# Partial maxima of two octets folded by one transposition in every odd slot, instead of one each slot

## The chip, the core and the metric

One Trainium2 chip, of which the kernel uses one core. The metric is the device time of one launch in microseconds (us), on the slowest core, here the only one. A core has five engines that run their own instruction lists and wait for one another on semaphores: TensorE (PE in the profile, with its weight loads as PEld), VectorE (DVE), ScalarE (ACT), GpSimd (POOL) and SyncE (SP, which here only issues DMAs; SPq and ACTq are the DMA issues of SP and ScalarE).

## The reference

Sixteen batches of 128 rows and 1024 columns pass through a gated cross attention and a gated feed-forward layer with low-rank experts. Cut to what matters here:

```python
def reference(x, ctx, ...):
    # x, ctx: (16, 128, 1024) float32
    y = layernorm(x)
    q, k, v = proj(y, Wq, bq), proj(ctx, Wk, bk), proj(ctx, Wv, bv)   # (b, 16 heads, 128, 16, 4)
    q, k, v = interfere(q), interfere(k), interfere(v)                # mixes the 4 parts of a head
    scores = einsum('bhqdm,bhkdm->bhqkm', q, k) / sqrt(16)            # 64 (head, part) pairs a batch
    weights = softmax(scores, axis=3)                                 # over the 128 keys
    out = einsum('bhqkm,bhkdm->bhqdm', weights, v)
    x = x + tanh(g_xattn) * (out.reshape(b, s, dm) @ Wo.T + bo)
    return x + tanh(g_ffn) * ffn(layernorm(x))                        # base product + 8 experts of rank 64
```

## The kernel before

**The program as a whole.** Three stages follow one another, all bound by matmuls. First the projections of keys, values and queries (up to about 523 us of the profiled execution), then attention (about 523 to 930 us), then the feed-forward part. Each product of two float32 matrices is made of three matmuls of rounded halves (hi by hi, hi by lo, lo by hi).

**Octets and slots.** The 64 (head, part) pairs of a batch are handled in octets of eight, so there are `OCTS` = 128 octets. Attention is written as a row of slots, and each engine has its own loop over the slots `s`. What an engine does for octet `o` stands in a fixed slot: TensorE makes the first scores and the fold of octet `s` in slot `s`, and the second scores of octet `s - LAG` with `LAG` = 3.

**Why scores are made twice.** Softmax needs the maximum over keys, but scores stand with keys on partitions. So:

- `first_pass(o, i)` (line 1734) makes the scores of half `i` of an octet, two matmuls into PSUM bank `one_bank[i]`. `first_pass(s + 1, 0)` is issued in slot `s`, `first_pass(s, 1)` at the start of slot `s`.
- VectorE's `partial_max(o, i)` (line 1924) turns 32 by 32 squares of it and takes negated maxima into the tile `part`, 16 numbers a partition for each half (s_part).
- TensorE's `fold(o)` (lines 1738 to 1742) waits for both halves and transposes `part` into the first 32 rows of `one_bank[1]`, 32 rows by 128 columns. VectorE's read of the fold (lines 1961 to 1966) reduces them into `negmax`, one number for each of 32 by 32 (s_max). The next octet's `first_pass(s + 1, 1)` writes the same bank, and so waits for s_max.
- GpSimd (lines 2017 to 2026) splits `negmax` into a hi and a lo row in `neg`: a copy (line 2022) and a subtraction (line 2024).
- SP's `place_max(o)` (lines 1644 to 1647) stands in slot `o + 1` and copies `neg` into two further rows of the octet's query tile by DMA (s_neg). Behind it, in each slot, SP issues `load_oct(s + 4)`, three DMAs of keys and queries, and in early slots stores of late queries and loads of `wo` rows.
- `second_pass(o)` (line 1754) makes the scores again with those two rows, so that the maximum is subtracted inside the matmul, four matmuls into `two_bank`. It waits for s_neg and, for each bank, for ScalarE's exponentials of the octet before (line 1870).

**What else TensorE does in a slot.** Every fourth slot (7, 11, 15 to 131, all odd, called values slots below; `half_at(s, 0)` is not None) it issues `values(h)` (line 1771), 64 small matmuls. In the other slots from 16 on it issues `project` (lines 1715 to 1717): two, three and three groups of three matmuls in the three slots between values slots, none in a values slot itself. Slots up to 15 have `late_step` (lines 1784 to 1786) instead: the last five of the query projections' 40 steps each, which the kernel has moved into attention. ScalarE and VectorE evict each late block (lines 1853 and 1957) in slots 3, 6, 9, 13 and 16 (`late_end` + 1), and SP and ScalarE store it. In VectorE's loop the late eviction stands ahead of the read of the fold.

**Order in a slot on TensorE.** In a values slot: `first_pass(s, 1)`, `values`, `first_pass(s + 1, 0)`, `fold(s)`, `second_pass(s - 3)`. In the others: `first_pass(s, 1)`, the first half of the projection or late work, `second_pass(s - 3)`, `first_pass(s + 1, 0)`, `fold(s)`, the rest of that work.

## Time and profile before

| | |
|---|---|
| time, median of 3 runs | 1318.53 us |
| lowest and highest | 1314.94 and 1320.28 us |
| the profiled execution: time | 1313.11 us |
| its span (first to last instruction) | 1311.3 us |
| TensorE matmul busy | 1294.1 us, 99% |
| VectorE, ScalarE, GpSimd busy | 57%, 31%, 48% |

The profile is of one execution. Its busy shares are averages over three stages. A busy TensorE is no TensorE at its peak, since the duration of a matmul contains the time in which the next one already runs; what a matmul costs is the distance to the next. The chain of waits gives that distance for each piece of work. TensorE's granted clock is at full speed (its upper level, 2.4 GHz) throughout attention. Idle time of an engine that nobody waits for costs nothing.

### The profile page before, as it was taken

How to read it: one execution, taken by the hardware profiler on the slowest of the kernel's cores; microseconds unless marked ns; L12 is line 12 of the kernel's file. 1: busy time of each engine (PE TensorE's matmuls, PEld its weight loads, DVE VectorE, ACT ScalarE, POOL GpSimd, SP SyncE). 2: the span in 40 equal slices, each digit the busy share in tenths (PEclk: the TensorE clock that was granted, in tenths of full speed). 3: DMA queues.
4: the chain of work that ended last, by engine and by line, in shares of the span. 5: the costliest groups of instructions: out<-in, count | busy, mean ns of one | idle time of the engine just before them, and what ended most of it. 6: DMA issues, size and time to landing. Idle time of an engine off the chain costs nothing.

```text
span 1311.3 us, 22186 instructions
## 1 busy us (share of the span) xinstructions
PE 1294.1 (99%) x8128; PEld 1087.0 (83%) x8128; DVE 742.2 (57%) x1375; ACT 411.2 (31%) x743; POOL 635.4 (48%) x801
## 2 busy tenths in 40 slices
PE   8999999999999999999999999999999999999999
PEld 8888888888878888787888888888788888888887
DVE  6423343468875546576777777777966355254100
ACT  3312221111112222455655555555550121111100
POOL 1899999999962641456665665655600000000000
PEclk9999999999999999999999999999999999999999
DMA  7898764467559997998878878777554514233011
GB/s 248 253 323 212 205 145 146 163 202 211 166 195 245 254 218 214 282 270 249 235 236 231 234 234 223 221 219 222 186 208 95 163 31 121 106 74 104 33 49 48
DMA packets 248077, 244.98 MB, mean 187 GB/s; under 512 B 81568, under 2 KB 182048, under 8 KB 247968
## 3 DMA queue, kind: packets, MB, share of 16 engines
q1 hardware_dynamic: 202416, 196.99, 51.3%
q10 hardware_dynamic: 45552, 46.56, 13.1%
q8 instruction: 65, 1.06, 0.3%
q14 instruction: 44, 0.36, 0.1%
HBM read 152.23 MB, written 83.90 MB: 180 GB/s over the span
## 4 chain that ended last, share of the span: by engine, by line
PE 66%; DMA 2%; ACTq 1%; SPq 1%; ACT 1%; issue 0%; DVE 0%; POOL 0%; DVEq 0%; POOLq 0%
PE bank L171 13%; PE bank L173 13%; PE bank L172 13%; PE bank L1734 5%; PE bank L1754 4%; PE bank L1715 4%; PE bank L1716 4%; PE bank L1717 4%; PE bank L1771 4%; PE bank L1741 1%; ACTq L695 1%; DMA wait_rows<-in_wo_rows 1%; DMA xb<-in_x 1%; DMA q_rows<-wq_own 0%; DMA q_in<-neg 0%
## 5 line engine op out<-in xcount | busy, mean ns | idle before, releaser
L1924 DVE TRANSPOSE_TENSOR_REDUCE part<-bank 128x16 f32<-128x512 f32 x256 | 174.2, 692 | 2.9 <-PE bank L1734 0.5
L1870 ACT ACTIVATE probT<-bank 128x512 f32<-128x512 f32 x256 | 138.8, 595 | 88.3 <-PE bank L1754 84.8
L1715 PE MATMUL bank<-w_hi,oT_hi 128*128 128x512 f32 x256 | 108.1, 422 | 1.2 <-POOL oT_lo L2037 1.2
L729 DVE SCALAR_TENSOR_TENSOR stage_lo<-bank,bias_mixed,stage_hi 128x512 fp32r<-128x512 f32 x46 | 34.5, 751 | 127.1 <-ACT stage_hi L731 127.1
L171 PE MATMUL bank<-place_a,w_hi 128*128 128x512 f32 x256 | 99.7, 390 | 1.7 <-DVE place_a L164 1.7
L1716 PE MATMUL bank<-w_lo,oT_hi 128*128 128x512 f32 x256 | 100.5, 392 | 0.0
L1717 PE MATMUL bank<-w_hi,oT_lo 128*128 128x512 f32 x256 | 100.3, 392 | 0.0
L171 PE MATMUL bank<-w_hi,yT_hi 128*128 128x512 f32 x256 | 99.9, 390 | 0.0
L173 PE MATMUL bank<-w_hi,yT_lo 128*128 128x512 f32 x256 | 99.6, 389 | 0.0
L172 PE MATMUL bank<-place_a,w_hi 128*128 128x512 f32 x256 | 99.6, 389 | 0.0
L172 PE MATMUL bank<-w_lo,yT_hi 128*128 128x512 f32 x256 | 99.6, 389 | 0.0
L173 PE MATMUL bank<-place_a,w_lo 128*128 128x512 f32 x256 | 99.6, 389 | 0.0
L171 PE MATMUL bank<-place_b,place_a 128*128 128x512 f32 x256 | 99.6, 389 | 0.0
L172 PE MATMUL bank<-place_c,place_a 128*128 128x512 f32 x256 | 99.6, 389 | 0.0
L173 PE MATMUL bank<-place_b,place_a 128*128 128x512 f32 x256 | 99.6, 389 | 0.0
L958 POOL TENSOR_TENSOR mixed_sum<-mixed_sum,mixed_part 128x512 f32<-128x512 f32 x64 | 90.8, 1419 | 5.0
L1538 DVE SCALAR_TENSOR_TENSOR raw_d<-bank,gates,raw_d 128x512 f32<-128x512 f32 x32 | 23.9, 746 | 121.2 <-PE bank L173 121.2
L2022 POOL CAST neg<-negmax 32x32 fp32r<-32x32 f32 x128 | 26.0, 203 | 133.4 <-DVE negmax L1965 84.9
L1965 DVE TENSOR_REDUCE negmax<-bank 32x32 f32<-32x128 f32 x128 | 35.7, 279 | 96.2 <-PE bank L1741 96.2
L171 PE MATMUL bank<-place_b,w_hi 128*128 128x512 f32 x216 | 84.5, 391 | 0.0
L172 PE MATMUL bank<-place_b,w_hi 128*128 128x512 f32 x216 | 84.1, 389 | 0.0
L173 PE MATMUL bank<-place_b,w_lo 128*128 128x512 f32 x216 | 84.1, 389 | 0.0
(256 smaller groups left out, 3123.5 us busy)
## 6 DMA issues: line engine op xcount, KB each, us to landing
k_rows<-stage_hi SPq DMA_DIRECT2D x128, 128.0 KB, 2.7
v_pad<-v_out SPq DMA_DIRECT2D x32, 512.0 KB, 2.8
v_place<-v_pad ACTq DMA_DIRECT2D x64, 256.0 KB, 4.2
tin<-in_ctx_cols SPq DMA_DIRECT2D x26, 512.0 KB, 4.0
k_in<-k_rows SPq DMA_DIRECT2D x64, 192.0 KB, 3.0
q_in<-q_rows SPq DMA_DIRECT2D x128, 96.0 KB, 3.3
q_rows<-wq_own SPq DMA_DIRECT2D x81, 128.0 KB, 4.2
raw_d<-x_mid SPq DMA_DIRECT2D x17, 512.0 KB, 3.6
```

The lines of the kernel that those rows point to most:

```text
L171: nc.tensor.matmul(bank_ap, sh, mh, start=(i == 0), stop=False)
L172: nc.tensor.matmul(bank_ap, sh, ml, start=False, stop=False)
L173: last = nc.tensor.matmul(bank_ap, sl, mh, start=False, stop=(i == len(chunks) - 1))
L958: then(pool.tensor_tensor(mixed_sum[:] if m < 3 else cols, mixed_sum[:], mixed_part[:], ALU.add))
L1715: pe.matmul(o_bank[out][:], hi[:, c, :], wo_hi[:, k, cols], start=(k == 0), stop=False)
L1716: pe.matmul(o_bank[out][:], hi[:, c, :], wo_lo[:, k, cols], start=False, stop=False)
L1717: last = pe.matmul(o_bank[out][:], lo[:, c, :], wo_hi[:, k, cols], start=False, stop=(k == KC - 1))
L1734: last = pe.matmul(dst, k_in[slot][0:ROWS, p, :], q_in[slot][0:ROWS, :, p, :], start=True, stop=True, skip_group_check=True)
L1754: last = pe.matmul(dst, k_in[slot][:, p, :], q_in[slot][:, :, p, :], start=True, stop=True, skip_group_check=True)
L1771: last = pe.matmul(v_bank[a][32 * p:32 * p + 32, i * P:(i + 1) * P], v_in[b % 2][:, 4 * (o % NOCT) + p, a, :], probT[o % NPT][:, p // 2, a ...
L1870: act.activation(probT[o % NPT][:, i].rearrange("k a p q -> k (a p q)"), two_bank[i][:], ACT.Exp).then_inc(s_exp, 1)
L1924: dve.tensor_reduce(part[o % NS][:, :, 2 * i:2 * i + 2, :].rearrange("k a p b -> k a (p b)"), one_bank[i][:].rearrange("k (a b t) -> k a b ...
```

## The change

Four edits, all in attention.

- `part` holds two octets, `[P, 2, 2, 4, 4]` in three buffers. `fold` runs in odd slots alone: one transposition of 64 columns for octets `s - 1` and `s`, into the first 64 rows of `one_bank[1]`. VectorE reads both in the odd slot, one reduction for each octet (the second reads rows 32 to 63), and GpSimd splits both there. SP places both in the even slot behind it, ahead of that slot's `load_oct`.
- `first_pass(o, 1)` of an odd octet waits for the partial maxima of the octet before (s_part), that of an even octet for the reads of the fold (s_max), both of them.
- In odd slots that are no values slots, `second_pass` stands behind `first_pass(s + 1, 0)` and `fold(s)` rather than ahead of them.
- VectorE's late eviction stands behind the reads of the fold.

```diff
-            part = [sb(f"part{i}", [P, 2, 4, 4], F32, st) for i in range(NS)]
+            part = [sb(f"part{i}", [P, 2, 2, 4, 4], F32, st) for i in range(NPAIR)]
...
-                    if 1 <= s <= OCTS:
+                    if 2 <= s <= OCTS and s % 2 == 0:
+                        place_max(s - 2)
                         place_max(s - 1)
...
+                        elif o % 2:
+                            pe.wait_ge(s_part, 2 * o)
                         elif o:
                             pe.wait_ge(s_max, o)
...
                 def fold(o):
-                    if 0 <= o < OCTS:
+                    if o < OCTS and o % 2:
                         pe.wait_ge(s_part, 2 * o + 2)
-                        pe.transpose(one_bank[1][0:32, 0:P], part[o % NS][:].rearrange("k a p b -> k (a p b)"),
+                        pe.transpose(one_bank[1][0:64, 0:P], part[o // 2 % NPAIR][:].rearrange("k e a p b -> k (e a p b)"),
                                      ident[:]).then_inc(s_fold, 1)
...
-                    second_pass(s - LAG)
+                    folds = h is None and s % 2 == 1
+                    if not folds:
+                        second_pass(s - LAG)
                     if h is None:
                         first_pass(s + 1, 0)
                         fold(s)
+                    if folds:
+                        second_pass(s - LAG)
...
+                    for o in (s - 1, s) if s < OCTS and s % 2 else ():
+                        dve.wait_ge(s_fold, s // 2 + 1)
+                        if o >= NS:
+                            dve.wait_ge(s_nlo, o - NS + 1)
+                        mine = one_bank[1][32 * (o % 2):32 * (o % 2) + 32, 0:P]
+                        dve.tensor_reduce(negmax[o % NS][:], mine.rearrange("c (i q) -> c q i", i=4), AX.X,
+                                          ALU.min).then_inc(s_max, 1)
                     for j, e in enumerate(late_end):
...
-                    if s < OCTS:
-                        dve.wait_ge(s_fold, s + 1)
-                        if s >= NS:
-                            dve.wait_ge(s_nlo, s - NS + 1)
-                        dve.tensor_reduce(negmax[at][:], one_bank[1][0:32, 0:P].rearrange("c (i q) -> c q i", i=4), AX.X,
-                                          ALU.min).then_inc(s_max, 1)
```

GpSimd's loop changes as VectorE's does: the copy and the subtraction of octets `s - 1` and `s` in odd slots, none in even ones.

TensorE in a values slot, from the fold to the first scores of the next octet's second half. Here `bank7` is `one_bank[1]`, into which fold and first scores both write, `bank0` and `bank1` are `two_bank`; `q_in`, `early_q` and `first_q` are query tiles, `k_in`, `early_k`, `second_k` and `first_k` key tiles. Before:

```order
L1741 MATMUL bank7<-ident,part1 32x128 [waits s_part]
L1754 MATMUL bank0<-q_in4,k_in4 128x2x128 [waits s_exp,s_neg4]
L1754 MATMUL bank0<-q_in4,k_in4 128x2x128
L1754 MATMUL bank1<-q_in4,k_in4 128x2x128 [waits s_exp]
L1754 MATMUL bank1<-q_in4,k_in4 128x2x128
L1734 MATMUL bank7<-first_q,first_k 128x2x128 [waits s_max]
```

Now:

```order
L1745 MATMUL bank7<-ident,part0 64x128 [waits s_part]
L1758 MATMUL bank0<-q_in4,k_in4 128x2x128 [waits s_exp,s_neg4]
L1758 MATMUL bank0<-q_in4,k_in4 128x2x128
L1758 MATMUL bank1<-q_in4,k_in4 128x2x128 [waits s_exp]
L1758 MATMUL bank1<-q_in4,k_in4 128x2x128
L1738 MATMUL bank7<-first_q,first_k 128x2x128 [waits s_max]
```

Nothing moved here; the transposition is wider, and its wait s_max, four matmuls later, now counts two reads.

TensorE two slots later, in the odd slot that is no values slot, from its second half on. Here `bank6` is `one_bank[0]`. Now the order is

```order
L1738 MATMUL bank6<-early_q2,early_k2 128x2x128 [waits s_part,s_kq2]
L1738 MATMUL bank6<-early_q2,early_k2 128x2x128
L1745 MATMUL bank7<-ident,part1 64x128 [waits s_part]
L1758 MATMUL bank0<-q_in6,k_in6 128x2x128 [waits s_exp,s_neg6]
L1758 MATMUL bank0<-q_in6,k_in6 128x2x128
L1758 MATMUL bank1<-q_in6,k_in6 128x2x128 [waits s_exp]
L1758 MATMUL bank1<-q_in6,k_in6 128x2x128
L1717 MATMUL bank5<-w0_hi,oT_hi0 128x512 [waits s_y]
```

where the second scores stood ahead of all of these rows before.

SP, the placing of maxima (`neg`) among the loads of keys and queries. Before:

```order
L1646 DMA early_q3<-neg3 2x32x32 [waits s_nlo]
L212 DMA first_k<-k_rows 96x512 [waits s_two]
L215 DMA first_q<-q_rows 48x512 x2
L1646 DMA q_in4<-neg4 2x32x32 [waits s_nlo]
L212 DMA second_k<-k_rows 96x512 [waits s_two]
L215 DMA early_q1<-q_rows 48x512 x2
L1646 DMA q_in5<-neg5 2x32x32 [waits s_nlo]
```

Now:

```order
L1647 DMA q_in6<-neg4 2x32x32 [waits s_nlo]
L1647 DMA q_in7<-neg5 2x32x32 [waits s_nlo]
L212 DMA k_in4<-k_rows 96x512 [waits s_two]
L215 DMA q_in4<-q_rows 48x512 x2
L212 DMA k_in5<-k_rows 96x512 [waits s_two]
L215 DMA q_in5<-q_rows 48x512 x2
L1647 DMA first_q<-neg0 2x32x32 [waits s_nlo]
```

The even octet's placing moved behind one more slot's loads.

## Rows read from the trace of the kernel before

**Rows 1.** The page: busy us (share of the span) xinstructions, for each engine.
```profile
PE 1294.1 (99%) x8128; PEld 1087.0 (83%) x8128; DVE 742.2 (57%) x1375; ACT 411.2 (31%) x743; POOL 635.4 (48%) x801
```

**Rows 2.** Who waited for whom: TensorE from 522 to 620 us: total, times, longest.
```profile
PE bank L1734 <- DVE negmax L1965: 3.7, 3, 1.7
PE bank L1734 <- DMA q_in<-q_rows: 0.7, 1, 0.7
PE bank L1754 <- DMA early_q<-neg: 0.6, 2, 0.4
PE bank L1734 <- DVE part L1924: 0.5, 1, 0.5
```

**Rows 3.** Chain of waits, start us and us, from a values slot on.
```profile
701.23 0.43 PE bank L1734 x2
701.67 0.11 PE bank L1741
701.78 0.48 PE bank L1754 x4
702.26 0.40 PE bank L1734 x2
...
703.83 0.24 PE bank L1734 x2
704.07 0.11 PE bank L1741
704.18 0.23 PE bank L1715
```

**Rows 4.** One line's instructions, L1741: count, ns min/median/max, first and last start.
```profile
L1741 PEld LDWEIGHTS bank<-ident,part x128: 94/94/96, 526.1 to 917.9; 128*32 128x32 f32 x128
```

**Rows 5.** One line's instructions, L1754, as in group 4.
```profile
L1754 PEld LDWEIGHTS bank<-q_in,k_in x256: 186/190/203, 550.3 to 924.9; 98*128 98x128 f32 x128
```

**Rows 6.** Timeline in and behind a values slot: start us, us, instruction, [idle before <-releaser].
```profile
713.54 0.27 PE L1741 MATMUL bank<-ident,part 128*32 128x128 f32 x1
713.57 0.72 PE L1754 MATMUL bank<-first_q,first_k 98*128 98x256 f32 x4
714.18 0.51 PE L1734 MATMUL bank<-q_in,k_in 96*128 96x256 f32 x2
...
718.36 0.64 PE L1754 MATMUL bank<-early_q,early_k 98*128 98x256 f32 x4
```

**Rows 7.** The same timeline on VectorE.
```profile
713.85 0.28 DVE L1965 TENSOR_REDUCE negmax<-bank 32x32 f32<-32x128 f32 x1 [1.06 <-PE bank L1741]
714.06 1.39 DVE L1924 TRANSPOSE_TENSOR_REDUCE part<-bank 128x16 f32<-128x512 f32 x2
```

**Rows 8.** Timeline on SP's queue, early slots and the stretch of group 6.
```profile
544.38 0.54 SPq L1646 DMA_DIRECT2D q_in<-neg  x1
...
547.26 0.54 SPq L1646 DMA_DIRECT2D q_in<-neg  x1
...
714.90 0.53 SPq L1646 DMA_DIRECT2D early_q<-neg  x1
```

**Rows 9.** DMA issues: KB each, median us from issue to landing.
```profile
v_place<-v_pad ACTq DMA_DIRECT2D x64, 256.0 KB, 4.2
...
yin<-yturn SPq DMA_DIRECT2D x144, 32.0 KB, 1.9
```

**Rows 10.** Chain of waits in early slots: start us, us.
```profile
537.26 0.75 DVE wq_own L1957
538.01 0.20 DVE negmax L1965
538.25 0.51 PE bank L1734 x2
...
551.77 4.30 DMA q_in<-neg
556.12 0.74 PE bank L1754 x4
```

**Rows 11.** Timeline on TensorE at the end of slot 16.
```profile
579.76 0.40 PE L1717 MATMUL bank<-w_hi,oT_lo 128*128 128x512 f32 x1
581.78 0.50 PE L1734 MATMUL bank<-early_q,second_k 96*128 96x256 f32 x2 [1.63 <-DVE negmax L1965]
```

More of the change, by code:

```diff
@@ L1149, in build @@
             NS = 6
-            part = [sb(f"part{i}", [P, 2, 4, 4], F32, st) for i in range(NS)]
+            NPAIR = NS // 2
+            part = [sb(f"part{i}", [P, 2, 2, 4, 4], F32, st) for i in range(NPAIR)]
             negmax = [sb(f"negmax{i}", [32, 32], F32, st) for i in range(NS)]
@@ L1923, in partial_max @@
                     dve.wait_ge(s_one, 2 * o + i + 1)
-                    dve.tensor_reduce(part[o % NS][:, :, 2 * i:2 * i + 2, :].rearrange("k a p b -> k a (p b)"),
+                    dve.tensor_reduce(part[o // 2 % NPAIR][:, o % 2, :, 2 * i:2 * i + 2, :].rearrange("k a p b -> k a (p b)"),
                                       one_bank[i][:].rearrange("k (a b t) -> k a b t", a=2, t=32), AX.X, ALU.max,
@@ L1930, in _ @@
                     if s < OCTS:
-                        at = s % NS
                         partial_max(s, 0)
@@ L2016, in _ @@
                 for s in range(SLOTS):
-                    if s < OCTS:
-                        at = s % NS
-                        pool.wait_ge(s_max, s + 1)
-                        if s >= NS:
-                            pool.wait_ge(s_neg[(s - NS) % KQ], 16 * ((s - NS) // KQ + 1))
+                    for o in (s - 1, s) if s < OCTS and s % 2 else ():
+                        at = o % NS
+                        pool.wait_ge(s_max, o + 1)
+                        if o >= NS:
+                            pool.wait_ge(s_neg[(o - NS) % KQ], 16 * ((o - NS) // KQ + 1))
                         pool.tensor_copy(neg[at][0:32], negmax[at][:]).then_inc(s_nhi, 1)
-                        pool.wait_ge(s_nhi, s + 1)
+                        pool.wait_ge(s_nhi, o + 1)
                         pool.tensor_tensor(neg[at][32:64], negmax[at][:], neg[at][0:32].bitcast(F32),
                                            ALU.subtract).then_inc(s_nlo, 1)
-                        pool.wait_ge(s_nlo, s + 1)
+                        pool.wait_ge(s_nlo, o + 1)
                     h = half_at(s, 5)
```

## The prediction, made before the changed kernel ran

> **What bounds the kernel now.** I read the busy shares first. TensorE has work in 99% of the span, VectorE in 57% [rows 1], so whatever moves the end must lengthen or shorten TensorE's own row of instructions. Then I read who waited for whom: nearly all of TensorE's visible waiting in attention lies before 620 us and sums to some 6 us [rows 2]. Last I read the chain of waits, since a busy share hides two things here. It prices each piece by the distance to the next: a fold costs TensorE 0.11 us, the two matmuls of a half of the first scores 0.24 us, the four of the second scores 0.48 us, a projection matmul 0.23 us. And in a values slot the two matmuls behind the second scores cost 0.40 us instead of 0.24 [rows 3]. That is a wait of 0.16 us which the table of waits doesn't show, because the matmul in front still counts as busy. It is the wait for the read of the fold. The reader should see two things: 128 folds, all on the path, and a wait behind the fold in every values slot that is already not covered.
>
> **Folds removed.** 64 of 128 folds go, at 0.11 us each [rows 3]: 64 x 0.11 = -7.0 us. All of it is on the path, as the chain runs through TensorE there.
>
> **Folds widened.** The remaining 64 load 64 columns instead of 32. The load of 32 columns takes 94 ns [rows 4], that of 128 takes 190 ns [rows 5], so one column costs 1 ns and 64 columns take about 126 ns. It runs beside the matmul in front, which lasts 0.12 us (half of 0.24). So between nothing and 0.03 us each, 0 to 2.0 us in all. I take 0.01 us, which is what sticks out of the cover: +0.6 us.
>
> **The wait in the values slots.** The fold starts at 713.54, TensorE goes on with the next first scores at 714.18 [rows 6]. In between VectorE starts its read at 713.85, needs 0.28 us, and is done at 714.13 [rows 7]. All that TensorE has to do meanwhile is the second scores, 0.48 us, and these don't cover it. Now the same first scores wait for two reads. VectorE's next instruction starts 0.21 us behind the start of a read [rows 7], so the second read ends 0.21 us later at least; if it begins only when the first is done, 0.28 us later. The second reads rows 32 to 63 of the bank, and no instruction in these slots changes rows like that, so no row decides between the ends; I take 0.24 us. Values slots with a next octet are 7 to 123, thirty of them, less slot 15 where a late step of 0.7 us lies behind the fold: 29 x 0.24 = +7.0 us (6.1 to 8.1). This eats what the folds give. The Trainium skill, in "VectorE: DVE Perf Modes", section "Two Vector instructions with no wait between them", states that an instruction whose input starts in another group of 32 partitions than the last one's is held until all earlier ones are finished. By that rule the upper end, 8.1 us, would be the value, and the sum 1.1 us higher; no row here shows it.
>
> **The other odd slots.** There the second scores now stand behind the fold. The read pair needs 0.31 us from the fold's start, 0.21 to 0.28 more, 0.28 and 0.05 us, some 0.9 us. Its cover is the fold, 0.11, the second scores, 0.48, and one group of three projection matmuls, 0.69 us: 1.28 us. So nothing; without the move the cover would be 0.80 us and a tenth would stick out. The fold itself comes 0.48 us earlier, and VectorE's partial maxima of the slot end more than that ahead. Even slots have no fold to wait for. Their first scores wait for partial maxima that are long made. Nothing.
>
> **Placing.** Even octets are placed one slot later. GpSimd's work per pair is the same. SP issues two DMAs in the even slot, 0.53 us each [rows 8], before that slot's loads, and none in the odd one. The loads are needed four slots on (12 us), so their delay is hidden. The window that shrinks is that of the even octets. For those folded in a plain odd slot the second scores come behind all of `values`, 1.9 us of work, so they keep over 5 us. For those folded in a values slot: fold at 713.54, placing issued at 714.90 [rows 8], that is 1.36 us behind; the second scores two slots on start at 718.36 [rows 6], 4.82 us behind the fold. After the change these are later by 0.24 (the longer wait) + 0.24 + 0.11 (first scores and fold put ahead) and earlier by 0.11 (the fold gone in between): 5.30 us. 5.30 - 1.36 = 3.9 us for landing, less 0.1 for the weight load: 3.8 us. What does landing take? Small pieces on the same queue take 1.9 us, and 256 KB on ScalarE's queue 4.2 us [rows 9]; this very DMA took 4.30 us in an early slot [rows 10]. With 26 such slots from 620 us on, the ends are 0 and 26 x 0.5 = 13 us. I take a landing mostly below 3.8 us, because the last load ahead of it on SP's queue is now issued some 3 us before instead of just before, with an occasional longer one: +1.5 us. The Trainium skill, in "DMA: Bandwidth & Descriptors", section "Anatomy of one DMA", gives a fixed cost of about 2.0 us for a DMA (fitted on GpSimd's path) and hardly anything for 8 KB. By that this term would be nothing and the sum 1.5 us lower; the 4.30 us of the row speaks against it for a loaded queue.
>
> **Early slots.** Two visible waits are for a read that stands behind a late eviction: 1.7 us before 538.25, behind VectorE's 0.75 us eviction that itself waited for ScalarE [rows 10], and 1.63 us before 581.78 [rows 11]. The first goes nearly whole, as the reads move ahead of the eviction. In slot 16 there is no fold any more, but the eviction still stands ahead of slot 17's partial maxima, so some 0.3 us remains. A short wait of the first fold for partial maxima goes too. But the early slots are also where SP is slowest: placings come 2.9 us apart there [rows 8], behind loads and stores, and octet 6's landing already holds TensorE up to 556.12 [rows 10]. Octets 4, 6, 16 and 18 would be placed 2 to 3 us later than now. What TensorE gains at 538 it then waits for at 550, and about 1 us more; again some 0.8 us at 556 and 1.5 us around 592 to 600. Sum of this part: -1.7 - 0.2 + 2.6 + 0.8 - 1.4 + 1.3 = +1.4 us. The ends: all waits of these slots that the edits touch go and nothing comes, -4 us; each of the four octets costs 2.5 us net of a gain of 4, +6 us.
>
> **Sum.** -7.0 + 0.6 + 7.0 + 0 + 1.5 + 1.4 = +3.5 us. Lower ends together: -7.0 + 0 + 6.1 + 0 + 0 - 4 = -5 us. The profiled execution took 1313.1 us, 5.4 us below the median of the runs shown (1314.9 to 1320.3). On its own time that is 1316.6 us, on the median 1318.5 + 3.5 = 1322 us.
>
> **The rivals.**
>
> *The placings land too late (slower).* Mechanism: in the slot two behind each values slot TensorE stands before the second scores until the even octet's maxima have landed. It speaks for it that engines of the DMA are mostly busy in attention and that 4.30 us was seen; against it that in the steady slots no wait for `neg` is listed now. At 4.3 us in all of them: 3.5 - 1.5 + 13 = +15 us, 1333.5 us. It leaves the band of no change when those 26 slots wait 0.18 us each on average, a mean landing near 4.0 us.
>
> *The wider fold costs by its columns (slower).* If the fold's 0.11 us is all its own columns, 64 cost 0.22 us and nothing is saved: +3.5 + 7.0 = +10.5 us, 1329 us. Against it: the load of 32 columns, 94 ns, already fits under the matmul in front, and 128 columns follow each other at 0.12 us [rows 3, 5].
>
> *The second read doesn't hold TensorE (faster).* If the pair ended no later than the one read now, or the second scores covered it, the folds' 7.0 us would stay: -7.0 + 0.6 + 0 + 1.5 + 1.4 = -3.5 us, and with the early waits gone as well (-4 instead of +1.4, no late landing) -10.4 us: 1308 to 1315 us. Against it: the chain shows this wait open already, so anything behind it is added.
>
> **How the numbers follow.** A measurement can tell about 0.5%, 6.6 us, from no change: 1311.9 to 1325.1 us. My sum lies inside it, chance 0.57. Late landings 0.23 and the costly fold 0.07 lie above it: 0.30 slower. The last rival far enough to leave the band, with the early waits gone: 0.13 faster. The range leaves out 0.1 at each side: it reaches down to 1312, where the lower ends of all terms lead (-5) and a little beyond, and up to 1334, the full price of the late landings.
>
> **What would show it.** Chain of waits in a values slot: the two matmuls behind the second scores at 0.61 to 0.68 us instead of 0.40. The fold at 0.11 or 0.12 us, 64 times. Two reads with starts 0.21 (or 0.28) us apart. No chain piece through VectorE's eviction at 538 us, but longer pieces of `neg` DMAs at about 550, 556 and 592 to 600 us. In steady slots hardly any wait of line 1758 for `neg`. Wrong would be: a stage much shorter than now by 5 us or more, which would mean that the second read is covered, or waits for `neg` in most of the slots behind a values slot.

## The result

| | median | lowest to highest | runs |
|---|---|---|---|
| before | 1317.21 us | 1314.53 to 1322.11 | 20 |
| after | 1321.92 us | 1318.55 to 1326.70 | 20 |

The ratio is 1.0042, with a 95% interval of 1.0031 to 1.0053: 0.4% slower, 4.7 us by the medians. Forecast was 1322 us and no change that counts, and both held. The sum of +3.5 us was near, but it was made of terms that were not all right: the trace shows two of them too small and two too large.

**The profile after.** The profiled execution took 1321.57 us (span 1319.7). The one of before took 1313.11 us and so lies 4 us below its own median, this one at its median. The two traces therefore differ by 8.4 us where the medians differ by 4.7.

The page's busy times of the changed kernel, against [rows 1]: 64 matmuls fewer on TensorE, and the same busy time.

```profile
PE 1294.2 (98%) x8064; PEld 1085.4 (82%) x8064; DVE 756.3 (57%) x1375; ACT 411.2 (31%) x743; POOL 635.0 (48%) x801
```

The difference can be divided at four marks: the start of the first first-scores and the folds of slots 23, 27 and 123. In TensorE's timeline of before they stand at 522.99, 605.20, 617.25 and 906.17 us. In that of after (L1738 and L1745, the fold now 64 columns wide):

```profile
522.87 0.64 PE L1738 MATMUL bank<-first_q,first_k 96*128 96x256 f32 x4
...
610.20 0.27 PE L1745 MATMUL bank<-ident,part 128*64 128x128 f32 x1
...
622.33 0.27 PE L1745 MATMUL bank<-ident,part 128*64 128x128 f32 x1
...
913.74 0.27 PE L1745 MATMUL bank<-ident,part 128*64 128x128 f32 x1
```

The first 24 slots take 87.3 us instead of 82.2: +5.1. The 24 cycles of four slots behind take 291.4 instead of 288.9 us: 12.14 instead of 12.04 us each, +2.5 in all. The slots at the end of attention and all behind them make +0.8.

**The steady part.** The chain of waits of after, from a values slot on, against [rows 3]:

```profile
706.99 0.43 PE bank L1738 x2
707.42 0.12 PE bank L1745
...
707.88 0.29 DVE negmax L1966
...
708.22 0.51 PE bank L1738 x2
708.73 0.23 PE bank L1717
...
712.44 0.24 PE bank L1738 x2
712.68 0.11 PE bank L1745
712.79 0.47 PE bank L1758 x4
713.27 0.23 PE bank L1717
```

From the fold to the first projection matmul: 708.73 - 707.42 = 1.31 us, which is the fold 0.12, the second scores 0.48 and 0.71 for the two first scores. In [rows 3] the same stretch is 0.11 + 0.48 + 0.40 = 0.99 us. So the wait behind the fold grew from 0.16 to 0.47 us, by 0.31 in each values slot, and the chain now goes through VectorE's second read. VectorE's timeline shows why, against [rows 7]:

```profile
707.57 0.59 DVE L1966 TENSOR_REDUCE negmax<-bank 32x32 f32<-32x128 f32 x2 [1.12 <-PE bank L1745]
708.20 1.31 DVE L1932 TRANSPOSE_TENSOR_REDUCE part<-bank 128x16 f32<-128x512 f32 x2
```

The two reads start 0.31 us apart: the second begins once the first is done. The fold of 64 columns costs 0.11 or 0.12 us like that of 32, and in the plain odd slot (712.44 on) nothing waits.

**The early slots.** Who waited for whom, TensorE from 520 to 612 us, against [rows 2]:

```profile
PE bank L1758 <- DMA early_q<-neg: 4.2, 1, 4.2
PE bank L1758 <- DMA q_in<-neg: 2.4, 1, 2.4
PE bank L1758 <- DMA first_q<-neg: 1.3, 2, 1.1
...
PE bank L1738 <- DVE negmax L1966: 0.4, 2, 0.2
```

The wait for the read of the fold is 0.4 us instead of 3.7, as the late eviction now stands behind it. The wait for landed maxima is 7.9 us instead of 0.6. The chain shows the two long ones:

```profile
546.21 5.18 DMA q_in<-neg
...
551.44 1.20 PE bank L1758 x4
...
596.03 5.70 DMA early_q<-neg
...
601.77 0.74 PE bank L1758 x4
...
603.96 0.43 PE bank L1717
604.39 0.43 PE bank L1718
```

These are octets 4 and 18, both even, both placed a slot later than before; the third wait, 1.1 us before 592.4, is octet 16's. The chain gives the time from issue to landing. By the semaphore events of the two traces, octet 4's DMA took 5.9 us before and takes 5.2 now, octet 16's 4.5 and 3.5, octet 18's 3.5 and 5.7. So only octet 18's took longer; the other two landed late because they were issued later (at 546.21 instead of 544.38, and at 588.86 instead of 586.02) and had nothing to spare: before, they landed 0.1 and 0.2 us ahead of their second scores.

The last two rows show a second price: a projection matmul costs 0.43 us instead of 0.23. Four stretches of after, the two waits and what came behind each (us, PE busy, PEclk in parts of full speed, DMA share of the 16 engines, GB/s):

```profile
549.00:552.00 3.00, 0.59 (x3) 0.92 0.85 245
552.00:555.00 3.00, 3.00 (x11) 0.52 0.77 223
597.60:602.20 4.60, 0.43 (x4) 1.00 1.01 302
602.70:606.10 3.40, 3.40 (x11) 0.50 0.77 230
```

Behind each long wait (2.4 us before 551.44 and 4.2 us before 601.77) TensorE ran at its lower level, 1.2 GHz, for 3.4 us. As an estimate from 0.43 and 0.23 us a matmul that costs some 1.6 us each time: of the 5.1 us some 3.2 are the clock's.

### The profile page after: what moved, and what is told of

It reads as the page before. It is cut to its first block, busy times and chain, and to the rows that moved or that the text cites. A ratio compares the mean times of both kernels' runs of the same rounds, so it can differ in the third digit from the quotient of the medians.

```text
span 1319.7 us, 22016 instructions
## 1 busy us (share of the span) xinstructions
PE 1294.2 (98%) x8064; PEld 1085.4 (82%) x8064; DVE 756.3 (57%) x1375; ACT 411.2 (31%) x743; POOL 635.0 (48%) x801
## 4 chain that ended last, share of the span: by engine, by line
PE 65%; DMA 2%; issue 1%; ACTq 1%; POOL 1%; DVE 1%; ACT 1%; SPq 0%; POOLq 0%; DVEq 0%
PE bank L171 13%; PE bank L173 13%; PE bank L172 13%; PE bank L1738 5%; PE bank L1775 4%; PE bank L1717 4%; PE bank L1718 4%; PE bank L1719 4%; PE bank L1758 3%; ACTq L695 1%; DVE negmax L1966 1%; DMA early_q<-neg 1%; PE bank L1745 1%; DMA xb<-in_x 0%; DMA q_in<-neg 0%
## 5 line engine op out<-in xcount | busy, mean ns | idle before, releaser
L1932 DVE TRANSPOSE_TENSOR_REDUCE part<-bank 128x16 f32<-128x512 f32 x256 | 179.3, 711 | 45.5 <-PE bank L1738 40.4
L1717 PE MATMUL bank<-w_hi,oT_hi 128*128 128x512 f32 x256 | 102.0, 398 | 1.1 <-ACT gated L1828 0.9
L958 POOL TENSOR_TENSOR mixed_sum<-mixed_sum,mixed_part 128x512 f32<-128x512 f32 x64 | 90.7, 1418 | 5.0
L173 PE MATMUL bank<-place_b,w_lo 128*128 128x512 f32 x216 | 84.1, 389 | 0.0
L172 PE MATMUL bank<-place_b,w_hi 128*128 128x512 f32 x216 | 84.1, 389 | 0.0
L731 ACT ACTIVATE stage_hi<-bank,bias_mixed 128x512 fp32r<-128x512 f32 x46 | 31.7, 689 | 163.0 <-PE bank L173 158.1
```

The source lines that it names most:

```text
L172: nc.tensor.matmul(bank_ap, sh, ml, start=False, stop=False)
L173: last = nc.tensor.matmul(bank_ap, sl, mh, start=False, stop=(i == len(chunks) - 1))
L958: then(pool.tensor_tensor(mixed_sum[:] if m < 3 else cols, mixed_sum[:], mixed_part[:], ALU.add))
L1717: pe.matmul(o_bank[out][:], hi[:, c, :], wo_hi[:, k, cols], start=(k == 0), stop=False)
L1932: dve.tensor_reduce(part[o // 2 % NPAIR][:, o % 2, :, 2 * i:2 * i + 2, :].rearrange("k a p b -> k a (p b)"), one_bank[i][:].rearrange("k ( ...
```

## The experiments

All on one core as above; ratios are to the kernel before, measured beside each. "Early" is the first first-scores to the fold of slot 23, "cycle" the mean of 24 cycles of four slots, from the fold of slot 27 to that of slot 123. Both are read at the same marks as above, in each kernel's one profile; a difference of a us or two in "early" is more than one profile can settle. "Low" is how many us of "early" had the granted clock at its lower level.

| kernel | median | ratio (95%) | early | low | cycle |
|---|---|---|---|---|---|
| before | | 1 | 82.2 | 0 | 12.038 |
| after | 1321.9 | 1.0042 (1.0031 to 1.0053) | 87.3 | 6.8 | 12.142 |
| late eviction alone | 1315.7 | 0.9988 (0.9977 to 0.9999) | 81.0 | 0 | 12.053 |
| placing in pairs alone | 1322.3 | 1.0044 (1.0028 to 1.0060) | 90.7 | 13.7 | 12.051 |
| before, folds twice | 1329.6 | 1.0090 (1.0072 to 1.0108) | 84.1 | 0 | 12.494 |
| after, late eviction ahead | 1324.3 | 1.0052 (1.0032 to 1.0071) | 84.9 | 3.4 | 12.141 |
| after, second scores ahead | 1333.2 | 1.0127 (1.0108 to 1.0145) | 92.1 | 13.7 | 12.407 |
| after, two folds into the same rows | 1327.0 | 1.0070 (1.0052 to 1.0087) | 87.3 | 6.8 | 12.243 |
| after, one read | 1317.9 | 1.0008 (0.9995 to 1.0021) | 85.8 | 10.2 | 11.852 |
| after, one read, second scores ahead | 1319.4 | 1.0021 (1.0007 to 1.0036) | 88.8 | 10.2 | 11.904 |
| after, early octets single | 1318.9 | 1.0013 (1.0000 to 1.0026) | 82.2 | 3.4 | 12.142 |
| both repairs | 1310.7 | 0.9946 (0.9931 to 0.9962) | 81.4 | 3.4 | 11.851 |
| both repairs and more cover | 1307.9 | 0.9939 (0.9916 to 0.9962) | 81.1 | 0 | 11.773 |

By the same estimate a us at the lower level costs 0.47 us. So much of what "early" differs by is the clock's: the 85.8 us of the kernel with one read would be some 81 without it.

### What a fold is worth

```diff
                 def fold(o):
                     if 0 <= o < OCTS:
                         pe.wait_ge(s_part, 2 * o + 2)
+                        pe.transpose(one_bank[1][0:32, 0:P], part[o % NS][:].rearrange("k a p b -> k (a p b)"), ident[:])
                         pe.transpose(one_bank[1][0:32, 0:P], part[o % NS][:].rearrange("k a p b -> k (a p b)"),
                                      ident[:]).then_inc(s_fold, 1)
```

> The kernel before with every fold issued twice into the same place, the second one releasing VectorE: it prices a fold of 32 columns. Theory: all 128 folds lie on the path at 0.11 us each: +14 us, 1330 us, ratio 1.0107, and four steady slots take 12.04 + 0.44 = 12.48 us. Rival: part of a fold lies in slack that other waits leave (in the values slots the read is waited for anyway), so that a fold is worth less than 0.11 us there: +7 to +11 us. The first would say that the 7.0 us for the 64 removed folds are real, the second that they were counted too high.

The median is 12.1 us above before's; the interval, 9.5 to 14.2 us, holds the theory and the upper part of the rival. The cycle decides: it takes 12.494 us, 0.456 / 4 = 0.114 us a fold. The chain shows both folds at their full price in a values slot, with the wait of 0.16 us behind them unchanged (the read only starts with the second):

```profile
712.44 0.11 PE bank L1741
712.55 0.11 PE bank L1742
712.66 0.48 PE bank L1755 x4
713.14 0.40 PE bank L1734 x2
```

So a fold is on the path in every slot. What taking one away gives back can be read from the kernel with one read, below, whose values slot is that of before: its cycle has two folds less and is 12.038 - 11.852 = 0.186 us shorter, 0.093 us a fold, 6.0 us for 64.

### Why the reads are 0.31 us apart

One kernel keeps the two reads, but brings both octets' maxima into the same 32 rows:

```diff
-                        pe.transpose(one_bank[1][0:64, 0:P], part[o // 2 % NPAIR][:].rearrange("k e a p b -> k (e a p b)"),
-                                     ident[:]).then_inc(s_fold, 1)
+                        for e in range(2):
+                            last = pe.transpose(one_bank[1][0:32, e * P:(e + 1) * P],
+                                                part[o // 2 % NPAIR][:, e].rearrange("k a p b -> k (a p b)"), ident[:])
+                        last.then_inc(s_fold, 1)
...
-                        mine = one_bank[1][32 * (o % 2):32 * (o % 2) + 32, 0:P]
+                        mine = one_bank[1][0:32, P * (o % 2):P * (o % 2) + P]
```

> The changed kernel, but a pair is folded by two folds of 32 columns into two different column ranges of the same 32 rows, so that both reads take their input from rows 0 to 31. Theory: the second read starts 0.31 us behind the first in the changed kernel because its input stands in another group of rows (the Trainium skill, in VectorE: DVE Perf Modes, section Two Vector instructions with no wait between them, says so). Here the reads should start 0.21 us apart, and the wait in the values slots fall from 0.47 to 0.37 us; with 64 more folds at 0.11 us: +7.0 - 2.9 = +4.1 us against the changed kernel, 1326 us. Rival: two reads of the bank follow each other at 0.3 us whatever their rows (the write of the first must be done, or the reduction itself takes that long): starts 0.31 apart, +7.0 us, 1329 us.

VectorE's timeline of this kernel:

```profile
709.94 0.48 DVE L1968 TENSOR_REDUCE negmax<-bank 32x32 f32<-32x128 f32 x2 [1.23 <-PE bank L1746]
```

The pair takes 0.48 us from start to end instead of 0.59. Over the 47 pairs of the steady part the starts are 0.207 to 0.209 us apart, where the changed kernel has 0.309 to 0.311 in all of its 48. A cycle costs 12.243 us: 0.10 more than the changed kernel's, which is 0.23 for two more folds, and 0.13 less of waiting (0.10 was expected). By the ratios the kernel is 3.7 us slower than the changed one, where 4.1 were expected.

The two reads here also lie in other columns than those of the changed kernel. But the step back from rows 32 to 63 costs the same: in the changed kernel VectorE's next instruction, which reads another bank from row 0 on, starts 0.311 to 0.314 us behind the second read, and in the kernel before 0.207 to 0.209 us behind its read of rows 0 to 31. This is the held instruction of the Trainium skill ("VectorE: DVE Perf Modes", section "Two Vector instructions with no wait between them"): with the same operation, shapes and waits, the group of 32 rows decides between 0.21 and 0.31 us.

### One read instead of two

```diff
-                    for o in (s - 1, s) if s < OCTS and s % 2 else ():
+                    if s < OCTS and s % 2:
                         dve.wait_ge(s_fold, s // 2 + 1)
...
-                        mine = one_bank[1][32 * (o % 2):32 * (o % 2) + 32, 0:P]
-                        dve.tensor_reduce(negmax[o % NS][:], mine.rearrange("c (i q) -> c q i", i=4), AX.X,
+                        dve.tensor_reduce(negmax[s // 2 % NPAIR][:], one_bank[1][0:64, 0:P].rearrange("c (i q) -> c q i", i=4), AX.X,
                                           ALU.min).then_inc(s_max, 1)
```

GpSimd's two operations of an odd octet then take rows 32 to 63 and put their hi row into that half of `neg`, the lo row into the other; the matmul adds both, so their order is free.

> The changed kernel, but one VectorE reduction of 64 rows by 128 columns reads both octets of a fold instead of two of 32 rows each. GpSimd's two operations per octet stay; for the odd octet they take rows 32 to 63. Theory: in the values slots TensorE waits for the end of the second read. With one read of the same 128 columns this wait falls from 0.47 to about 0.16 us: 29 x 0.31 = -9 us against the changed kernel, 1313 us, four slots in 11.83 us instead of 12.14. Rival one: a read of 64 rows takes twice as long as one of 32 (0.56 instead of 0.28 us): 29 x 0.03 = -1 us. Rival two: the 0.31 us are not the read at all but the placing or the matmuls themselves: no change.

The read of 64 rows takes no longer than that of 32, and the values slot is back to [rows 3]:

```profile
706.66 0.28 DVE L1965 TENSOR_REDUCE negmax<-bank 64x32 f32<-64x128 f32 x1 [1.12 <-PE bank L1745]
```

```profile
706.52 0.11 PE bank L1745
706.63 0.48 PE bank L1758 x4
707.11 0.41 PE bank L1738 x2
```

A cycle is 0.29 us shorter than in the changed kernel, 7.0 us in the 24. The median moved by 4 us only, where 9 were expected; the intervals of the two ratios allow 2 to 7. The steady part is near what was expected. The early slots, which in this kernel still place in pairs, were at the lower clock for 10.2 us of its profile, against 6.8 in the changed kernel's; whether that holds for its other executions isn't shown. With those repaired as well (below) the one read is worth 0.9946 against 1.0013, some 9 us.

### The second scores behind the fold

```diff
-                    folds = h is None and s % 2 == 1
+                    folds = False
```

> The changed kernel with one part undone: in the odd slots without values the second scores stand ahead of the fold, as before. Theory, with the two reads 0.31 us apart as the changed kernel's trace shows: the pair ends 0.31 + 0.31 + 0.28 + 0.05 = 0.95 us behind the fold's start, and the cover is the fold and one group of three projection matmuls, 0.80 us; 0.15 us sticks out in some 30 slots: +4.5 us against the changed kernel, 1326 us, and the two matmuls of the first scores' second half show 0.35 to 0.40 us there instead of 0.24. Rival: those slots have slack, and the order is worth nothing: 0 us, or below it by the shorter wait for the partial maxima.

This part of the change is needed, and by more than expected (4.5 us): a cycle takes 0.265 us more (it has one plain odd slot), some 8 us in all, and the kernel 11 us. Most of the rest fits the early slots, 4.7 us longer in its profile, with 13.7 us at the lower clock instead of 6.8. The chain in a plain odd slot, from the fold (0.11 us) to the first scores behind the three projection matmuls, 0.48 us instead of 0.24:

```profile
723.09 0.11 PE bank L1745
...
723.91 0.48 PE bank L1738 x2
```

The same with one read tests the sum that follows from it:

> The changed kernel with one read of 64 rows for a pair, and the second scores ahead of the fold again in the odd slots without values. It tests a sum that three kernels suggest: from the start of a fold to the end of its read 0.31 + 0.28 + 0.05 = 0.64 us, and 0.12 us more for the weight load of the first scores, which cannot run ahead of the wait: 0.76 us of cover are needed. Here the cover is the fold and three projection matmuls, 0.80 us: nothing sticks out, four steady slots take 11.85 us as with one read alone, 0 us. With two reads the same sum gives 1.07 - 0.80 = 0.27 us (0.26 seen). Rival: the second scores must stand behind the fold in any case: +0.26 us in each of these slots, 12.1 us for four, +8 us.

Here a cycle takes 11.904 us, 0.05 more than with one read alone, not 0.26. So the sum holds: from the fold's start to the read's end 0.64 us with one read and 0.95 with two, and 0.12 us more. For these the trace has a candidate, the load of the first scores' weights: in the changed kernel it starts only when the wait is over, at 708.22 us, while the next weights are loaded ahead, 0.11 us before their matmul starts at 708.56. No kernel changes this alone.

```profile
708.22 0.30 PEld L1738 LDWEIGHTS bank<-first_q,first_k 96*128 96x128 f32 x2 [0.42 <-DVE negmax L1966]
708.45 0.19 PEld L1717 LDWEIGHTS bank<-w_hi,oT_hi 128*128 128x128 f32 x1
```

Cover of 0.80 us is enough for 0.76 and short of 1.07 by 0.27 (0.265 seen); the fold and the second scores, 0.59 us, are short of 0.76 by 0.17 (0.16 seen) and of 1.07 by 0.48 (0.47 seen). The 0.05 us are a small wait elsewhere, which I have not followed. In both kernels with the second scores ahead, the early slots cost some us more than in their counterparts. Standing ahead, the second scores come 0.35 us earlier and need their maxima sooner; whether that is the cause was not tried.

### Where the early slots lose

Four kernels take parts of the change by themselves or out of it. The late eviction alone, in the kernel before:

```diff
+                    if s < OCTS:
+                        dve.wait_ge(s_fold, s + 1)
...
                     for j, e in enumerate(late_end):
                         if s == e + 1:
                             dve.wait_ge(s_lhi, j + 1)
...
-                    if s < OCTS:
-                        dve.wait_ge(s_fold, s + 1)
```

> The kernel before with one part of the change alone: the late query eviction stands behind the read of the fold. Theory: the two waits for the read that stood behind the eviction (2.0 us at 538, 1.9 us at 581) go, and nothing here is placed later, since every octet is still placed in the slot behind its fold: -2 to -4 us, ratio 0.997 to 0.9985; the steady part stays at 12.04 us for four slots. Rival: the next thing is nearly as late (the landing of the maxima), so that at most 1 us of it is left: ratio 0.999 to 1.000.

It is a small gain, 0.12%, with an interval (0.01 to 0.23%) that just leaves out zero. The waits for the read are gone, and others stand in their place, TensorE from 522 to 620 us:

```profile
PE bank L1754 <- DMA early_q<-neg: 2.9, 3, 1.3
PE bank L1754 <- DMA q_in<-neg: 0.7, 1, 0.7
```

With 0.6 us for `first_q` the waits for landed maxima are 4.2 us instead of 0.6. So most of the 3.7 us of [rows 2] was only the first of two things that were late. The early part is 1.2 us shorter, near the rival's 1 us.

The placing in pairs alone, in the kernel before:

```diff
                 for s in range(SLOTS):
-                    if 1 <= s <= OCTS:
+                    if 2 <= s <= OCTS and s % 2 == 0:
+                        place_max(s - 2)
                         place_max(s - 1)
```

> The kernel before with one part of the change alone: SyncE places the maxima of two octets in every even slot, those of the even octet a slot later; folds, reads and the late eviction stand as before. Theory: this alone makes the loss of the first 24 slots, in which the DMA engines are busy 94% of the time and landings take up to 5.7 us: the second scores of octets 4, 16 and 18 wait 1.4 to 4.4 us for their maxima. +3 to +6 us, ratio 1.002 to 1.0045; the first 24 slots take about 86 us instead of 82, the steady part stays at 12.04 us for four slots. Rival: the loss comes from the pair of reads or from the folds, which end later, and the placing has slack: ratio 0.999 to 1.001.

This alone makes a kernel as slow as the changed one, with folds, reads and eviction as before. The steady cycle is that of before within 0.013 us: there the later placing costs nothing. All the loss is early, 8.5 us in this profile, where 4 were expected:

```profile
PE bank L1755 <- DMA early_q<-neg: 3.9, 2, 3.5
PE bank L1755 <- DMA first_q<-neg: 2.8, 2, 1.7
```

These are the waits of octets 10 and 18, and 0 and 16. Octet 4, which was expected among them, landed 3.8 us ahead of need. Again the clock is low around the long waits, for 13.7 us in all, some 6.4 of the 8.5 us by the estimate above (columns as above; the wait for octet 18's maxima and the stretch behind it):

```profile
600.20:604.20 4.00, 0.55 (x2) 0.85 1.00 280
605.50:609.80 4.30, 4.30 (x14) 0.50 0.64 184
```

The changed kernel with the first 24 octets folded, read and placed one per slot:

```diff
+            SINGLE = 24
...
-                    if 2 <= s <= OCTS and s % 2 == 0:
+                    if 1 <= s <= SINGLE:
+                        place_max(s - 1)
+                    elif s <= OCTS and s % 2 == 0 and s:
                         place_max(s - 2)
                         place_max(s - 1)
...
-                    if o < OCTS and o % 2:
+                    if o < SINGLE:
+                        pe.wait_ge(s_part, 2 * o + 2)
+                        pe.transpose(one_bank[1][0:32, 0:P], part[o // 2 % NPAIR][:, o % 2].rearrange("k a p b -> k (a p b)"),
+                                     ident[:]).then_inc(s_fold, 1)
+                    elif o < OCTS and o % 2:
```

> The changed kernel, but the first 24 octets are folded, read and placed one per slot as in the kernel before (the late query eviction stays behind the read); the pairs begin with octet 24. Theory: the 5.0 us that the changed kernel loses up to slot 23 come from placing octets 4, 16 and 18 a slot later. The waits of 2.9 and 4.4 us before their second scores go, and with them the two stretches at the lower granted clock behind them; 12 folds come back, 1.3 us, and 4 reads in values slots become single, -1 us. Against the changed kernel -5 us, 1317 us; slot 23's mark at about 606 instead of 611 us. Rival: the landings there are late because the DMA engines are loaded, whatever the time of placing, and the waits only move: 0 to -1 us.

Early is 82.2 us, as before the change, and the cycle is 12.142 us to the last digit that of the changed kernel. The median fell by 3.0 us, by the ratios 3.8, less than the 5.1 of the profile and the 5 expected. What is left against before, 0.13% (0 to 0.26%, up to 3.4 us), has room for the 2.5 us of the steady part. One wait of 1.7 us for maxima is still there (before 595.89), with a fall of the clock behind it:

```profile
596.90:600.20 3.30, 3.30 (x10) 0.50 1.01 303
```

This kernel also undoes folds, reads and the order in the early slots; that the placing is what matters there rests on the kernel ahead of it.

And the late eviction ahead of the reads again, in the changed kernel:

```diff
+                    for j, e in enumerate(late_end):
+                        if s == e + 1:
+                            dve.wait_ge(s_lhi, j + 1)
...
                     for o in (s - 1, s) if s < OCTS and s % 2 else ():
...
-                    for j, e in enumerate(late_end):
```

> The changed kernel with one part undone: the late query eviction stands ahead of the two reads of the fold again. Theory: it matters only where a late step ends in an odd slot or the one before; the wait of about 2 us before the first scores of the slot after 537 us comes back, and the placing of that pair then comes later by as much. Against the changed kernel (1321.9 us) +1 to +3 us, so ratio to before 1.005 to 1.007. In the steady part nothing changes: 12.14 us for four slots. Rival: what TensorE gains at the reads it loses again before the second scores of octet 4, so the order makes no difference: 0 to +0.5 us.

Inconclusive: 1.0052 against 1.0042, intervals that overlap. In its profile TensorE waits for the read again, 0.7 us before 540.28, and 1.9 us before 537.81 for the load of a query tile, which is no part of this edit. The wait of 2.4 us at 549 us and the fall of the clock behind it are absent, so that early is 84.9 us, less than in the changed kernel. That fits the rival as far as it goes, that what TensorE gains at 538 us it gives back at 549 us; but one profile with a wait of another kind in it doesn't show it.

Why the landings in the early slots take up to 5.9 us, before the change too, was not tried by a run of its own. The rows show that the 16 DMA engines are at 1.01 of their time while TensorE waits (597.60 to 602.20 us above), and that the share is 0.94 in the early slots of the kernel before against 0.81 in the steady ones:

```profile
523.00:605.20 82.20, 76.01 (x690) 1.00 0.94 275
605.20:917.00 311.80, 311.80 (x3199) 1.00 0.81 229
```

### Both repairs, and more cover

Pairs only from octet 24 on, and one read for a pair:

> Both repairs together: pairs only from octet 24 on, and one VectorE reduction of 64 rows for both octets of a pair. Theory: the early part costs what it does in the kernel before (82 us from the first first-scores to the fold of slot 23), and four steady slots take 11.85 us instead of 12.04: 24 x 0.19 = -4.5 us to slot 123, -5 us with the last slots: about 1311.5 us where the kernel before takes 1316.3, ratio 0.996. Rival: the one-read kernel's time (0.9995 to 1.0021 of before) says that something outside these two parts gives the gain back; then 1315 us or more, ratio above 0.999.

Measured 1310.7 us, 0.9946 (0.9931 to 0.9962): 0.5% below the kernel before, early and steady part both as expected.

What stays is the wait of 0.16 us in the values slots, for want of 0.17 us of cover. A group of three projection matmuls ahead of the waiting first scores would be enough:

```diff
+                    ahead = s > SINGLE and len(work) > 1 and half_at(s - 1, 0) is not None
+                    if ahead:
+                        project(*work[0])
                     first_pass(s, 1)
...
-                    for part_of in work[:(len(work) + 1) // 2]:
+                    for part_of in work[1 if ahead else 0:(len(work) + 1) // 2]:
```

> The kernel with both repairs, and one group of three projection matmuls (0.69 us) ahead of the waiting half of the first scores in each slot behind a values slot. By the same sum 0.76 us of cover are needed there and 0.59 us stand there (the fold and the second scores), which leaves the wait of 0.16 us that the kernel before has too; with 1.28 us of cover it goes: 25 x 0.16 = -4 us against the kernel with both repairs, ratio to before 0.9915, four steady slots in 11.69 us. Rival: VectorE's partial maxima, now 0.69 us later in that slot, or the landing of the maxima hold TensorE instead, and the gain is given back: 11.85 us, ratio 0.9945 or more.

Half of it came: a cycle takes 11.773 us, 0.078 less, where 0.16 was expected. The chain behind a values slot:

```profile
700.69 0.48 PE bank L1765 x4
...
701.87 0.24 PE bank L1741 x2
702.11 0.56 PE bank L1765 x4
```

The first scores (701.87) no longer wait, 0.24 us. But the next second scores take 0.56 instead of 0.48. The third of their four matmuls costs 0.20 instead of 0.12: it needs a bank which ScalarE's exponentials of the octet before leave only at 702.11, behind the eviction of the values' bank, and its weight load starts at 702.17:

```profile
700.22 0.69 ACT L1881 ACTIVATE raw_s<-bank,side 128x512 f32<-128x512 f32 x1 [1.60 <-PE bank L1782]
...
701.52 0.59 ACT L1888 ACTIVATE probT<-bank 128x512 f32<-128x512 f32 x1
```

This is the next limit of that slot. The median, 1307.9 us, is the lowest of all; against the kernel without this step the ratios' intervals overlap, so only the trace shows its gain.

## Why the prediction was right, point by point

- **Folds removed, -7.0.** Right: 0.114 us each by the kernel that folds twice, 7.3 us; 0.093 each, 6.0 us, by the cycle of the kernel with one read.
- **Folds widened, +0.6.** Nothing: the chain has 0.11 or 0.12 us for 64 columns as for 32. The rival by columns is ruled out. (Its sum kept the +0.6 that it replaces; without it, it is +9.9 us.)
- **The wait in the values slots, +7.0.** Right in its mechanism and its place, too small in size: 0.31 us a slot instead of 0.24, 29 x 0.31 = +9.0. The mis-sized term is the distance between the two reads. The ends named were 0.21 and 0.28; the trace has 0.31, above the upper one, since 0.03 us lie between the end of the first and the start of the second. The Trainium skill's rule was the better guide here, and the middle value between it and the row of another pair the wrong choice. In a cycle -0.23 + 0.31 = +0.08 us; 0.104 was measured.
- **The other odd slots, 0.** Right. The aside that without the move "a tenth would stick out" was short: 0.27 us, as the weight load behind the wait was left out.
- **Placing in the steady slots, +1.5.** Nothing. For the octets of this term a landing takes 2.0 to 3.5 us and comes 0.5 us or more ahead of need (1.6 us before the change). The other even octets' take up to 4.6 us, the closest 0.2 us ahead. And the kernel that only places later has the same cycle as before. The rival of late landings was right in its mechanism, but its place was the early slots, not the 26 steady ones.
- **Early slots, +1.4 (-4 to +6).** The places were right: the wait at 538 us went, and waits at 549 us, 591 us and 597 us came. Octet 6, for which 0.8 us were set at 556 us, did not wait. The sizes were wrong: the early part is 5.1 us longer, of which 12 folds less are -1.4 and three longer waits in values slots +0.9, so the term is +5.6. Two steps failed. One is octet 18: its issue came 3.5 us later, within reach of the 2 to 3 us that were set, but its landing took 5.7 us instead of 3.5, and TensorE waited 4.2 us, where 1.5 us were set for octets 16 and 18 together; why this landing was slow stays open. Octet 4's wait, 2.4 us, was forecast well. The other is the lower clock behind the long waits, some 3.2 us, which was in no term. The waits listed grew by 3.3 us; with the clock that is 0.9 us more than the term, which I can't place.
- **The sum.** By the trace -7.3 + 0 + 9.0 + 0 + 5.6 = +7.3 us, and 1.1 us in small pieces make the 8.4 us between the two profiles. Against the medians (+4.7) it is too much, and the record of each execution's mean granted clock says a part of why. The profiled execution of before had 1.000; those of the kernel before beside the experiments, 61 of them, had 0.9976 on average, the twenty of the changed kernel 0.9964. That is 6.3 and 9.5 us at the lower level, 1.5 us of cost between them by the estimate above, where the two profiles differ by 3.2. The rest of the gap the runs leave open. The kernel with single early octets puts the early part at 3.8 us. That the forecast of +3.5 us came so near is luck: the errors had both signs.

The rival in which the second read doesn't hold TensorE is ruled out by the chain, where the second read stands, and by the kernel with one read, which is what that rival described: its cycle is 11.85 us.

## What to carry to other kernels

Cover is counted from the start of the producer to the end of the last reader, plus the weight load that can't run ahead of the wait; here 0.64 + 0.12 us, and 0.31 more for the second read. Of these the 0.12 us are inferred, and the sum was tested by one kernel beyond those it was made from. When two small pieces of work are merged on one engine, merge their reader too: the fold of two octets paid only when one reduction of 64 rows read it, for 0.28 us like one of 32. And a pair makes its first member late: look at what each transfer has to spare before it is needed. Here the octets that came to wait had 0.2 us or less before the change, the steady ones 1.6 us or more; merge only where there is such slack.

## What the runs showed of the hardware

- VectorE's two reads of 32x128 from PSUM start 0.31 us apart when they lie in different groups of 32 rows, 0.21 us apart in the same rows. A read of 64 rows takes 0.28 us, as one of 32.
- A transposition of 64 columns costs TensorE 0.11 us in its row, as one of 32.
- After waits of 2.4 and 4.2 us in attention the granted clock of the changed kernel was at its lower level (0.50 and 0.52 of full speed in the rows above) for 3.4 us each, and the matmuls cost 0.43 instead of 0.23 us. A wait is then dearer than it looks. Its length alone doesn't decide: in the kernel before two waits of 1.7 and 1.6 us were followed by full speed, in the kernel with single early octets one of 1.7 us by the lower level. The first of the kernel before, with columns as above:

```profile
536.50:538.70 2.20, 0.47 (x4) 1.00 1.04 312
538.70:542.00 3.30, 3.30 (x21) 1.00 0.67 202
```

- The start of attention lay between 522.9 and 528.2 us in the profiles of these kernels, though no edit touches anything before it. In seven of the thirteen profiles the granted clock was at its lower level for 3.4 us at about 377 to 382 us, in the projections, and in these attention starts at 525.1 to 526.2 us; four without it start at 522.9 to 523.1, but two others without it at 524.4 and 528.2. A comparison of two single profiles needs such marks, or several us are put down to the wrong cause.
